# A token part of five stages in a row becomes a pipeline of four chunks with a written list of steps

## What is computed

```
h = layernorm(h + attention(h))      # within each image: 64 tokens
h = layernorm(h + moe8(h))           # 8 experts of 64 -> 256 -> 64, top 1, a capacity for each expert
                                     # counted over all 4096 tokens in order
h = layernorm(h + mingru2(h))        # two recurrent layers along each image's 64 tokens
h = layernorm(h + moe16(h))          # 16 experts of 64 -> 128 -> 64, top 2, all computed,
                                     # with a layernorm, gamma and beta of its own
```

## Time and profile before

| | |
|---|---|
| median of three runs (3174.87 to 3186.03) | 3181.86 us |
| profiled execution: its own time, its span | 3175.57 us, 3173.6 us |
| token part in the span | from 2552.9 us to 3173.6 us |
| busy in the span: PE, DVE, ACT | 2792.6, 2076.7, 1994.0 us |
| mean granted TensorE clock | 0.96 |

### The profile page before, as it was taken

How to read it: one execution, slowest core, us unless ns; L and a number is a source line. 1 busy time by engine, 2 the same in 40 slices (tenths; PEclk the granted TensorE clock), 3 DMA queues, 4 the chain that set the end, 5 groups by cost and what they waited for, 6 DMA issues and landing times.

```text
span 3173.6 us, 77921 instructions
## 1 busy us (share of the span) xinstructions
PE 2792.6 (88%) x30128; PEld 1796.9 (57%) x30128; DVE 2076.7 (65%) x3890; ACT 1994.0 (63%) x2399; POOL 61.8 (2%) x81
## 2 busy tenths in 40 slices
PE   5777789999789998989998799999999969964994
PEld 3444466666566666666666444444444449952893
DVE  6999668888568887768886544544544442256457
ACT  6888666777557776656775477777777734422451
POOL 0000000000000000000000200000000001000000
PEclk9999999999999999999999999999999988986897
DMA  3422356645446544557455341111111000000000
GB/s 98 134 100 110 123 161 213 211 173 181 147 145 220 194 175 150 188 158 229 170 182 160 117 107 35 59 57 45 49 57 47 13 1 1 1 1 1 1 1 13
DMA packets 110789, 335.76 MB, mean 106 GB/s; under 512 B 46726, under 2 KB 74662, under 8 KB 74790
## 3 DMA queue, kind: packets, MB, share of 16 engines
q1 hardware_dynamic: 88102, 161.45, 16.2%
q10 hardware_dynamic: 18432, 134.23, 10.4%
q0 software_dynamic: 4096, 37.75, 5.6%
HBM read 179.24 MB, written 154.14 MB: 105 GB/s over the span
## 4 chain that ended last, share of the span: by engine, by line
PE 77%; DVE 9%; ACT 6%; issue 5%; DMA 2%; ACTq 0%; SPq 0%; DVEq 0%
PE pA L1295 15%; PE pT L1390 8%; PE pA L1303 8%; PE pS L1332 7%; PE pD L1379 4%; PE pD L1346 4%; PE pD L466 3%; PE pA L466 3%; PE pT L1321 3%; PE pD L1361 3%; PE pD L1266 3%; PE pT L458 2%; PE pS L458 2%; DVE arena L1662 2%; PE pA L1321 2%
## 5 line engine op out<-in xcount | busy, mean ns | idle before, releaser
L1629 DVE TENSOR_REDUCE small<-arena 128x32 f32<-128x1056 f32 x320 | 396.4, 1240 | 314.3 <-ACT arena L1464 311.9
L1295 PEld LDWEIGHTS pA<-conv_bd,h_in 128*128 128x128 f32 x4096 | 479.0, 192 | 107.5 <-issue 107.5
L1295 PE MATMUL pA<-conv_bd,h_in 128*128 128x128 f32 x4096 | 517.5, 280 | 2.0 <-DVE arena L1622 1.7
L1454 ACT COPY w_sb<-pA 128x1024 f32<-128x1024 f32 x256 | 259.4, 1013 | 248.9 <-PE pA L1303 231.8
L1475 ACT ACTIVATE h_new<-pT,bet,gam 128x1024 f32<-128x1024 f32 x256 | 307.1, 1200 | 153.4 <-PE pT L1321 134.1
L1643 DVE SCALAR_TENSOR_TENSOR w_sb<-w_sb,small 128x1024 f32<-128x1024 f32 x320 | 385.3, 1208 | 2.1
L1464 ACT ACTIVATE arena<-w_sb 128x1024 f32<-128x1024 f32 x320 | 338.6, 1058 | 10.2
L1332 PEld LDWEIGHTS pS<-cst,h_new 128*128 128x128 f32 x2048 | 222.4, 142 | 205.5 <-issue 134.6
L1321 PE MATMUL pT<-cst,w_sb 128*128 128x128 f32 x2048 | 277.4, 280 | 38.7 <-DVE w_sb L1643 19.3
L1332 PE MATMUL pS<-cst,h_new 128*128 128x128 f32 x2048 | 282.7, 282 | 25.4 <-ACT h_new L1475 22.9
L1321 PEld LDWEIGHTS pT<-cst,w_sb 128*128 128x128 f32 x2048 | 232.2, 144 | 104.0 <-DVE w_sb L1643 48.2
(11 more groups left out here) (299 smaller groups left out, 3794.7 us busy)
## 6 DMA issues: line engine op xcount, KB each, us to landing
h_scratch<-h_new ACTq DMA_DIRECT2D x128, 1024.0 KB, 4.4
h_in<-h_scratch SPq DMA_DIRECT2D x128, 1024.0 KB, 5.0
y_scratch<-w_sb POOLq DMA_DIRECT2D x32, 576.0 KB, 8.5
y_in<-y_scratch SPq DMA_DIRECT2D x512, 36.0 KB
w_sb<-in_L_tok_w1r_dram POOLq DMA_DIRECT2D x8, 576.0 KB, 6.8
w_sb<-in_L_tok_w1i_dram POOLq DMA_DIRECT2D x8, 576.0 KB, 6.9
w_sb<-in_L_tok_w2r_dram POOLq DMA_DIRECT2D x8, 576.0 KB, 7.2
w_sb<-in_L_tok_w2i_dram POOLq DMA_DIRECT2D x8, 576.0 KB, 6.8
```

Of the source, the lines that this page charges most:

```text
L1295: pe.matmul(pA[:, c:c + 128], h_in[:, 1024 * n + c:1024 * n + c + 128], conv_bd[:], start=(j == 0), stop=False, skip_group_check=True)
L1454: act.copy(raw[n], pA[:]).then_inc(s["copied"], 1)
L1629: dve.reduce_sum(var[n], sq[n % 2], axis=AX).then_inc(s["summed"], 1)
```

## The change

The 32 tiles are cut into four chunks of eight (1024 tokens, 512 columns of `X`). Every step of the token part is now written for one chunk, and one text, `TOKEN_ORDER`, gives the order of all steps, `step.chunk`. Each of the three engines walks the same list and does its own share of each step. A word `e1.c` or `e2.c` is one expert's two units for chunk c; the experts of a chunk follow one another as they come in the weights. `token_steps` puts the hidden products ahead of the outputs as far as eight buffers allow, across chunks too.

```diff
+TOKEN_ORDER = """
+    xt1.0 qkv.0 sc.0 ex.0 xt1.1 pt.0 qkv.1 pv.0 sc.1 ex.1 pt.1 wg.0 xt2.0 gl1.0 gx1.0 cum.0
+    e1.0 pv.1 xt1.2 qkv.2 e1.0 xt2.1 e1.0 sc.2 gl1.1 gx1.1 ex.2 e1.0 cum.1 e1.0 pt.2 pv.2 e1.0 gt1.0 xt1.3 qkv.3 e1.0 e1.0 eb1.0
+    e1.1 post1.0 sc.3 e1.1 ex.3 xt2.2 xt3.0 pt.3 e1.1 gru0.0 gl1.2 gx1.2 e1.1 gru1.0 cum.2 e1.1 gback.0 pv.3 e1.1 xt4.0 gl2.0 gx2.0
+    e1.1 gt1.1 gm2.0 e1.1 eb1.1
+    e2.0 post1.1 e2.0 e2.0 xt3.1 e2.0 gru0.1 e2.0 e2.0 gru1.1 e2.0 e2.0 gback.1 e2.0 gt2.0 e2.0 xt4.1 gl2.1 gx2.1 e2.0 xt2.3 gl1.3 gx1.3
+    e2.0 gm2.1 e2.0 cum.3 e2.0 e2.0 e2.0 eb2.0
+    e1.2 post2.0 e1.2 e1.2 e1.2 gt1.2 e1.2 e1.2 e1.2 e1.2 eb1.2
+    e1.3 post1.2 e1.3 xt3.2 e1.3 gru0.2 e1.3 gru1.2 e1.3 gback.2 e1.3 xt4.2 gl2.2 gx2.2 e1.3 gt1.3 gm2.2 e1.3 eb1.3
+    e2.1 post1.3 e2.1 e2.1 xt3.3 e2.1 gru0.3 e2.1 e2.1 gru1.3 e2.1 e2.1 gback.3 e2.1 gt2.1 e2.1 e2.1 xt4.3 gl2.3 gx2.3 e2.1 e2.1 gm2.3
+    e2.1 e2.1 e2.1 eb2.1
+    e2.2 post2.1 e2.2 e2.2 e2.2 e2.2 e2.2 e2.2 e2.2 e2.2 e2.2 e2.2 e2.2 gt2.2 e2.2 e2.2 e2.2 e2.2 eb2.2
+    e2.3 post2.2 e2.3 e2.3 e2.3 e2.3 e2.3 e2.3 e2.3 e2.3 e2.3 e2.3 e2.3 gt2.3 e2.3 e2.3 e2.3 e2.3 eb2.3
+    post2.3
+"""
...
+def token_steps():
...
+        for _ in range(2):
+            while issued < len(units) and units[issued][0:2] in split and held + slots(units[issued][0]) <= 8:
...
+                steps.append((f"hid{layer}", u, e, k, slot))
...
+            steps.append((f"out{layer}", u, e, k, at))
...
+            def taken(which, *key):
+                pe.wait_ge(s[f"t{which}_free"], mark[key][which] + 4)
...
+            def xt3(c):
+                pe.wait_ge(s["fed"], c + 1)
+                turn_x(c)
...
+            def xt4(c):
+                pe.wait_ge(s["recurred"], c + 1)
+                turn_x_twice(c)
...
+            def logits(E, gw, split):
+                def step(c):
+                    taken("d", split, c)
...
+            for key in token_steps():
+                if key[0] in do:
+                    do[key[0]](*key[1:])
+                mark[key] = dict(n)
...
+            def gx1(c):
+                act.wait_ge(s["e_subbed"], c + 1)
+                act.activation(exp1[c % 2], shifted1[c % 2], ACT.Exp).then_inc(s["e_exped"], 1)
...
+                    act.activation(GS, see(0)[:], ACT.Sigmoid, bias=gbias[:, 2 * layer + 1:2 * layer + 2]).then_inc(s["gru_act"], 1)
...
+            def layer_norm(x):
...
-                rsqrt_here(r, var)
+                link(dve.tensor_scalar(ln_r.bitcast(I32), ln_var.bitcast(I32), -0.5, float(0x5F3759DF), ALU.mult, ALU.add))
+                link(dve.tensor_tensor(ln_x, ln_r, ln_r, ALU.mult))
...
+            def lower(c):
+                for j in range(2):
...
+                    b = take()
+                    dve.wait_ge(s["upper"], lowered[0])
+                    dve.tensor_tensor(XT_split[64:128, a:a + 512].bitcast(F32R), b[64:128, :], XT_split[64:128, a:a + 512], ALU.subtract).then_inc(s["td_free"], 1)
...
-            pool.wait_ge(s["tok_ready"], 2)
+            pool.wait_ge(s["tok_ready"], 1)
...
+            for c in range(NCH):
+                sp.wait_ge(s["acc_done"], c + 1)
```

More of the change, by code:

```diff
@@ new lines @@
+"""
+TOKEN_SENDS = dict(xt1=(0, 2), qkv=(4, 2), sc=(1, 0), pt=(0, 2), pv=(1, 0), xt2=(2, 0), xt4=(2, 0), gl1=(1, 0), gl2=(1, 0), cum=(1, 0),
+                   wg=(0, 1), gt1=(0, 1), gt2=(0, 1), eb1=(1, 0), eb2=(1, 0), xt3=(0, 2), gru0=(1, 1), gru1=(1, 1), gback=(1, 0),
+                   hid1=(0, 2), hid2=(0, 1), out1=(1, 0), out2=(1, 0))
+def token_steps():
+    words = [(op, int(c)) for op, c in (w.split(".") for w in TOKEN_ORDER.split())]
+    units, seen = [], {}
+    for op, c in words:
+        if op in ("e1", "e2"):
+            e = seen.get((op, c), 0)
+            seen[op, c] = e + 1
+            units += [(int(op[1]), c, e, k) for k in range(2)]
+    slots = lambda layer: 2 if layer == 1 else 1
+    steps, split, held, issued, out, slot = [], set(), 0, 0, 0, 0
+    for op, c in words:
+        if op not in ("e1", "e2"):
+            steps.append((op, c))
+            if op in ("xt2", "xt4"):
+                split.add((1 if op == "xt2" else 2, c))
+            continue
+        for _ in range(2):
+            while issued < len(units) and units[issued][0:2] in split and held + slots(units[issued][0]) <= 8:
+                layer, u, e, k = units[issued]
+                units[issued] += (slot,)
+                steps.append((f"hid{layer}", u, e, k, slot))
+                held += slots(layer)
+                slot = (slot + slots(layer)) % 8
+                issued += 1
+            layer, u, e, k, at = units[out]
+            steps.append((f"out{layer}", u, e, k, at))
+            held -= slots(layer)
+            out += 1
+    return steps
@@ L447, in experts, with xt2 @@
[L447 to L453, removed]
+                pe.transpose(b[:, 0:P], wg0, ident)
+                sent("s", pe.transpose(b[:, P:2 * P], wg1, ident))
+            def xt2(c):
+                pe.wait_ge(s["attended"], c + 1)
+                turn_x_twice(c)
@@ L525, in token_pe, with gback @@
+            def gback(c):
+                pe.wait_ge(s["gru_out"], 2 * c + 2)
                 b = bank("d")
                 for i in range(4):
-                    t = 4 * j + i
-                    mm = pe.transpose(b[:, 128 * i:128 * i + 128], OUT1[:, 128 * t:128 * t + 128], ident)
+                    mm = pe.transpose(b[:, 128 * i:128 * i + 128], OUT1[:, 128 * i:128 * i + 128], ident)
                 sent("d", mm)
-            experts(4, **LAYER2)
+            do = dict(xt1=xt1, qkv=qkv, sc=sc, pt=pt, pv=pv, wg=wg, xt2=xt2, xt3=xt3, xt4=xt4, gl1=logits(E1, gwa, "xt2"), gl2=logits(E2, gwb, "xt4"),
+                      cum=cum, hid1=hidden(1, split="xt2", **LAYER1), hid2=hidden(2, split="xt4", **LAYER2), out1=output(1, **LAYER1), out2=output(2, **LAYER2),
+                      gt1=turn_gates(E1, gates1, "gated"), gt2=turn_gates(E2, gates2, "pair_gated"),
+                      eb1=output_bias(1, E1, GT1, b2a), eb2=output_bias(2, E2, GT2, b2b), gru0=gru0, gru1=gru1, gback=gback)
@@ L544, in token_act @@
+            do = dict(xt1=turn_x, xt3=turn_x, qkv=qkv, ex=ex, pt=pt, xt2=upper, xt4=upper, gx1=gx1, gx2=gx2, hid1=hidden(**LAYER1), hid2=hidden(**LAYER2),
+                      gt1=turn_gates(E1, GT1), gt2=turn_gates(E2, GT2), wg=wg, gru0=gru(0), gru1=gru(1))
             act.wait_ge(s["r_free"], 20 * NG + 2)
             act.sem_inc(s["tok_ready"], 1)
-            def turn_x():
-                for j in range(8):
-                    act.copy(XT[0:64, 512 * j:512 * j + 512], take()[0:64, :]).then_inc(s["ts_free"], 1)
@@ new lines, in post2 @@
+            def post2(c):
+                x, y = chunk(X, c), chunk(Y, c)
+                link(dve.tensor_tensor(y, y, x, ALU.add))
+                layer_norm(y)
+                link(dve.tensor_tensor(by_tile(y), by_tile(y), per_tile(gamma), ALU.mult))
+                link(dve.tensor_tensor(by_tile(y), by_tile(y), per_tile(beta), ALU.add))
+                link(dve.tensor_tensor(x, x, y, ALU.add))
+                layer_norm(x)
+                dve.sem_inc(s["acc_done"], 1)
+            do = dict(qkv=qkv, sc=sc, pv=pv, xt2=lower, xt4=lower, gl1=gl1, cum=cum, out1=combine(E1, gates1), out2=combine(E2, gates2),
+                      eb1=add_bias, eb2=add_bias, post1=post1, gru0=gru(0), gru1=gru(1), gback=gback, gl2=gl2, gm2=gm2, post2=post2)
```

689 lines of the change are left out of this document (357 added, 332 removed).

## The result

Before: 3181.86 us, median of three runs (3174.87 to 3186.03); a fourth, at 3333.52, fell in a slower state and is left out. After: 3225.01 us, median of four runs (3216.49 to 3232.21). The ratio is 1.0138, 95% interval 1.0098 to 1.0177: the kernel became slower by 1.4%, where 1.7% faster was forecast. The profiled execution of after took 3232.21 us, its span is 3230.4 us and its mean granted clock 0.938.

What follows compares the result with a forecast made beforehand. The prediction took PE, with the largest sum of work, plus waits between engines to bound the token part: 50 + 433 + 55 + 15 + 18 = 571 us against 620.7, hence 3129 us in all, range 3085 to 3165.

Steps and rivals of the forecast that it cites:

- PE's work, 433: Token part after its start: PE's full-clock work still to do, 433 us of 460 for four chunks.
- Waits on the way, 55: Token part between start and end: PE idle for late steps, mostly DVE's, 55 us in all.
- `xt3` of the four chunks: PE's turn behind the DVE step `post1` in each chunk: waits of 2.6, 5.4, 5.2 and 5.5 us.
- The closing norms: In e2.2 and e2.3, `post2` (13.3 us on DVE) against four output banks of 2.7: PE waits 3.5 us each.
- Start, 50, and end, 18: Token part: 50 us until the experts stand; 18 us after the last output for biases, `post2.3` and the store.
- DVE and ACT, 388 and 224: Token part, four chunks: summed work of 388 us on DVE and 224 on ACT, both below PE's 460.
- Table loads: ACT, token part: 11 exponential and sigmoid loads, 8 more than before, 10 us, nearly all taken as off the path.
- ACT holds up the experts (rival): ReLUs queue on ACT behind exponentials waiting for DVE: nine places, 3 us each, 27 on top, 3156; chance 0.15.
- the 30 named as a sign: Prediction called wrong if ReLUs wait behind ACT's exponentials for over 30 us in all.
- The clock, 15: Half clock behind nine gaps of 2.6 us or longer: 3.2 us each, 29 at most, half taken, 15.
- the prediction's signs of being wrong: PE idle outside start and end under 15 or over 90 us; second-mixture pitch well above 1.35; long ReLU waits.
- the third rival: Gaps and narrow products hold PE at half clock: second-mixture units 2.56 instead of 1.35, 3202 with 60; chance 0.10.

Runs made afterwards that it cites:

- e1: Not a follow-up run here: word of `TOKEN_ORDER` for one expert's two units of the first mixture, the digit behind the dot being the chunk; no time of its own.
- e2: Not a follow-up run here: word of `TOKEN_ORDER` for one expert's two units of the second mixture, the digit behind the dot being the chunk; no time of its own.

## Why the prediction was wrong

- **PE's work, 433: right.** 424.6 at full clock, 2% less.
- **Waits on the way, 55: near, and mostly in their places.** 49.0. `xt3` of the four chunks: walked 2.6, 5.4, 5.2 and 5.5, in sum 18.7; measured 13.3 + 5.5 = 18.8. The second gate of chunk 0: 8.7, measured 8.6. The closing norms: 3.5 each, measured 3.8 each, and none under e1.2. Not all of this is shown working: by the numbers that the prediction gives, `post2` leaves 13.3 - 4 x 2.7 = 2.5, not 3.5, and `xt3.1` 9.9 - 2 x 2.7 = 4.5, not 5.4; the measured waits bear out the larger numbers.
- **Start, 50, and end, 18:** 41.8, 8 less than walked, with PE busy for 27.1 us of it, and 17.2. The store took 2.6 us for each quarter, where 3 was taken.
- **DVE and ACT, 388 and 224:** 356 and 231 over these stretches; neither bounds.
- **Table loads: right.** 11, and on no path that PE waits on by more than 0.8 us. ACT's table loads of after, by line; two more lines have one load each:

```profile
L720 ACT ACT_TABLE_LOAD x5 | 6.4, 1283 | 2.1 <-PE pD L622 2.0
L694 ACT ACT_TABLE_LOAD x4 | 5.1, 1283 | 0.1
```

- **ACT holds up the experts (rival): no.** ACT did wait 41.8 us for DVE ahead of the two gates' exponentials, over the 30 named as a sign; but all waits of PE for ACT in the middle are 1.5 us.
- **The clock, 15: this step failed.** It was 137.4. The count of places was near: nine gaps predicted (its list has eleven entries of 2.6 us or longer), 13 falls measured, six of them at the narrow gate products. The price of one was wrong: 3.2 us at most, 1.7 as taken; measured 137.4/13 = 10.6. Two sentences carried the mistake. "Where the next wait is for DVE, PE's loss is taken back there" holds only if the loss ends at the next wait, and it went on behind it. And against the rival the prediction put "that the clock came back within 10 us with PE busy": read off, behind other products in the image part, and carried over to the expert stream. The second mixture's units didn't bring the clock back by themselves within 224 us of busy PE, as the one gap in the kernel before shows. One of the prediction's signs of being wrong came about with it: the pitch of these units, put at 1.35, was 2.56 in the long stretches (3111.00 to 3113.56 in the trace of after).

With 137.4 in place of 15, and the measured start, waits, work and end, the sum is 41.8 + 424.6 + 49.0 + 137.4 + 17.2 = 670.0. So what came about is the third rival, "the clock falls and stays", given 0.10; its price of 1.21 a unit stands, and its example of 60 units (3202) was still under the outcome. "e1.2, e2.2 and e2.3 have long stretches" was counted against it, and the long stretches of two of them hold the two largest losses: 28.6 and 25.6 us in e2.2 and e2.3.

The trace of the kernel before held the warning. Timeline of PE there, at the start of the first mixture and of the second:

```profile
2637.32 0.77 PE L458 MATMUL pS<-XT_split,w1a_hi 128*128 128x512 f32 x1
...
2641.73 0.59 PE L458 MATMUL pS<-XT_split,w1a_hi 128*128 128x512 f32 x1
2642.16 0.40 PE L458 MATMUL pS<-XT_split,w1a_lo 128*128 128x512 f32 x1
...
2940.13 0.77 PE L458 MATMUL pT<-XT_split,w1b_hi 128*128 128x512 f32 x1
...
2947.31 0.80 PE L458 MATMUL pT<-XT_split,w1b_hi 128*128 128x512 f32 x1 [3.42 <-ACT w_sb L569]
...
2956.01 1.08 PE L466 MATMUL pD<-spec,w_sb 128*128 128x64 f32 x8
2956.90 0.48 PE L458 MATMUL pS<-XT_split,w1b_hi 128*128 128x512 f32 x1
```

At the first, twelve hidden products stand in a row, and within them the clock rises. At the second, eight in a row stay at half clock, PE waits 3.42 us, eight more stay at half clock, and the rise comes only in the third unit behind them, at 2956.2. Such runs stand only at the head of each mixture, where the buffers are filled. From there on the clock held to the end of both stretches, so no row of the two showed what it takes to come back in mid-stream. The prediction read 1.00 as a property of the stream; for the second mixture the two runs with the gap in the kernel before show that it was one of what came ahead.

The stream of experts is not one thing in this, either. Timeline of PE in after, in the fall at chunk 1's gate:

```profile
2667.37 3.51 PE L592 MATMUL pA<-spec,w_sb 128*128 128x64 f32 x16
...
2672.49 2.53 PE L592 MATMUL pA<-spec,w_sb 128*128 128x64 f32 x16
```

The clock rises within the second row, with nothing but four hidden products and sixteen outputs in turn on PE since 2665.5. In the first mixture of after this happened three times, after 37.5, 17.1 and 27.3 us at half clock, with only such units on PE for the last 7 us or more. In the second mixture, with two hidden products and eight outputs in turn, the stretch behind `post2.1` ended only behind the product of the gates and biases (`eb2.2`), and the one behind `post2.2` lasted to the end of the experts. A short one, 6.8 us behind `gl2.3`, did end among its units.

What stays open: which feature of the expert stream keeps it in either state. The runs show that ten 512-column products in a row brought the clock back, that bunches of eight shorten the falls, and that gaps and narrow products drop it; eight in a row ahead of the second mixture of before didn't bring it back at once.

## What to carry to other kernels

A stall's price is its own time and what the clock does behind it: look for the next row at full clock, not for the end of the wait, and look in the trace for the same stream coming out of half clock by itself before the cost of a fall is put at a few microseconds. Where a kernel mixes wide and narrow products, issuing the wide ones in bunches added no idle time here and ended half-clock stretches early, and a DVE step that blocks PE's buffers is worth cutting in pieces even where the wait is under 4 us. A pipeline that interleaves small products into a stream trades idle time for the risk of half clock; count both columns.

## What the hardware showed beside that

PE can be busy for 224.12 of 224.80 us at a granted clock of 0.50, and the same 874 instructions take 119.33 us at 1.00; which of the two it is was decided by ten products ahead of them. The Trainium skill, "TensorE: Matmul & The Clock Gate", section "Why this matters for your kernels", advises to avoid idle gaps of PE between bursts: the trace agrees, at 28.6 us for a wait of 3.8. The Trainium skill, same page, section "What's actually happening", says that activity releases the throttle; the row of 224 us shows a busy engine for which it didn't. Here the measurement decides. And the clock fell behind products of 8 columns with PE busy for 10.40 of 10.40 us, where the same step at 64 columns kept it at all seven places that PE reached without a wait.
